# Low-rank attention: a row product in a key pair of banks ahead of the block of full products, and a fifth key tile that begins its chain afresh

## The chip, the cores and the metric

The program runs on one core of one Trainium2 chip. The metric is device microseconds of one execution. The engines are named PE (TensorE matmul), PEld (its weight loads), DVE (VectorE), ACT (ScalarE), POOL (GpSimd) and SP (SyncE, which here only issues DMAs).

## What is computed

The input x is (8, 1024, 128) in float32. Six residual layers follow one another, each after a layer norm:

```python
    x = x + 0.5 * _L0_ffn_ref(_layernorm(x, axis=-1), ...)
    x = x + _L0_attn_ref(_layernorm(x, axis=-1), ...)
    x = x + 0.5 * _L0_ffn_ref(_layernorm(x, axis=-1), ...)
    x = x + 0.5 * _L1_ffn_ref(_layernorm(x, axis=-1), ...)
    x = x + _L1_attn_ref(_layernorm(x, axis=-1), ...)
    x = x + 0.5 * _L1_ffn_ref(_layernorm(x, axis=-1), ...)
```

The change is in the fifth, the low-rank attention with 8 heads over 1024 positions in each of 8 batches. Its front, as the reference has it:

```python
        c_q = h_t @ W_DQ + b_DQ
        c_kv = h_t @ W_DKV + b_DKV
        q_c = (c_q @ W_UQ + b_UQ).reshape(b, s, N_HEADS, D_K).transpose(0, 2, 1, 3)
        k_c = (c_kv @ W_UK + b_UK).reshape(b, s, N_HEADS, D_K).transpose(0, 2, 1, 3)
```

After it come a softmax over all 1024 keys, the weighing of the values and the product with W_O. The kernel absorbs the key weights into the query, so that a score is a product over KR = 64 numbers (32 latent, 32 rotary), the same keys for all heads of a batch.

## The kernel before

The stages run in the order a, w, b, c, m, d, for the six layers; m is the low-rank attention. The work of stage m is written out as a plan by low_rank_plan: a list of steps g, eight for each of 64 units u (8 batches by 8 heads; "head" below). Every engine walks through the same plan (pe_low_rank, act_low_rank, dve_low_rank, pool_low_rank) and takes its part of each step; semaphores order the engines among themselves.

In step g = 8u + t the key tile t of head u is scored against all 1024 queries: pe_key_scores writes [128 keys x 1024 queries] into a key pair of banks, pair 0 for even and pair 1 for odd tiles (side 0 and side 1 are the two halves of the queries). act_exponentials takes the exponential of the pair, and a pair is free for tile g + 2 when that is done (key_exp). Products are split into high and low parts of f32r. Tiles 0 and 1 have four terms: key high by query high, key low by query high, key high by query low, and the shift, a row of ones by q_shift, which subtracts each query's maximum. Tiles 2 to 7 don't start the bank anew. They add to the scores of tile t - 2, still in the bank, the product with the difference of the two key tiles (step_high, and its low part in key_low), three terms, and the shift stays in.

The maxima come from row products: pe_row_scores multiplies 128 queries by 512 keys for each side into one of the pairs 2 and 3, and dve_row_max reduces the pair to two maxima per partition. Eight row products serve one head; row r is issued at step g = r - ROW_LEAD, thirteen steps ahead, one in each step. After the eighth, dve_row_top reduces them, pool_shift makes shift_cols of it on GpSimd, and SP moves that into q_shift by eight DMAs of 128 numbers (sync_move_shift). q_shift and shift_cols have one buffer each. SP's order is: set for head u, then the four transfers of o_norm of head u - 2 (sync_move_head), and a store of a batch once in eight heads. PE waits for the set at the fourth term of tile 0 (shift_ready).

At t = 3 (BURST) of each head the block of full products follows the key tile on PE: the query product of a head ahead, one or two items (projections, transposes, low-rank features, differences and so on), the totals of the head before (pe_totals) and its weighing (pe_weigh), and then the row product. Items, weighing and row products take the pairs 2 and 3 in turn; each waits until the use before the last of the list is done (pair_free). On DVE the order of that step is: q_low, first item, norm work, reciprocal of the totals, second item, o_norm, row maximum.

## Time and profile before

| what | value |
| --- | --- |
| median of 3 runs | 1689.36 us (1688.67 to 1693.62) |
| the profiled execution | 1689.08 us, its span 1687.2 us |
| PE busy | 1549.9 us (92%) |
| DVE busy | 1282.9 us (76%) |
| ACT busy | 1044.0 us (62%) |
| POOL busy | 1018.0 us (60%) |
| DMA queue of SP | 21.0% of the 16 engines |

The span is the profiled execution from first to last instruction; the run's own time has some 2 us around it. Stage m covers roughly 600 to 1650 us. In the timelines a row is a run of like instructions: start, duration, engine, line, operation, output and input tile, count, and in brackets how long the engine had been idle and what released it. A name's buffer number is left out, so "pair" stands for all four pairs of banks.

### The profile page before, as it was taken

The numbers are of one execution on the slowest core, as the hardware profiler recorded it, in microseconds if no ns is written. First come the engines' busy times: TensorE is split into PE (matmuls) and PEld (weight loads), VectorE is DVE, ScalarE is ACT, GpSimd is POOL, SyncE is SP. The second block draws the span as 40 slices with busy tenths as digits, with TensorE's granted clock in tenths as the row PEclk, the third lists the DMA queues.
The fourth block names the chain that finished last, engine by engine and source line by source line (L and its number), as shares of the span: only waits on it lengthen the run. The fifth ranks groups of instructions, "written<-read, shape, count | busy, mean of one in ns | idle before, by whom it ended". The sixth has DMA issues, their size and how long they took to land.

```text
span 1687.2 us, 42461 instructions
## 1 busy us (share of the span) xinstructions
PE 1549.9 (92%) x16971; PEld 1071.7 (64%) x16971; DVE 1282.9 (76%) x2345; ACT 1044.0 (62%) x1670; POOL 1018.0 (60%) x727
## 2 busy tenths in 40 slices
PE   4669999999987789999999999999999999999995
PEld 3557777777766546666666666666666666666664
DVE  5656777776669678788888888888887888887862
ACT  5447777778757436656665756656665666565562
POOL 5300111100026539778888888888888888887882
PEclk9879999999978779999999999999999999999998
DMA  4465566765200000000000010010010001001001
GB/s 132 119 165 143 144 163 154 177 149 151 60 30 1 1 1 11 10 9 11 8 12 10 9 23 9 11 20 12 8 24 9 10 10 22 11 8 23 8 12 44
DMA packets 198681, 81.63 MB, mean 48 GB/s; under 512 B 152552, under 2 KB 177492, under 8 KB 198356
## 3 DMA queue, kind: packets, MB, share of 16 engines
q1 hardware_dynamic: 198484, 78.93, 21.0%
q8 instruction: 133, 2.18, 0.6%
q14 instruction: 64, 0.52, 0.1%
HBM read 39.79 MB, written 29.88 MB: 41 GB/s over the span
## 4 chain that ended last, share of the span: by engine, by line
PE 58%; POOL 2%; DVE 2%; ACT 2%; issue 1%; SPq 0%; DMA 0%; ACTq 0%; DVEq 0%; POOLq 0%
PE pair L1930 23%; PE pair L1984 13%; PE pair L1859 7%; PE pair L1971 5%; PE pair L1676 2%; PE pair L1665 1%; ACT prob L1943 1%; DVE amax L1869 1%; PE pair L1690 1%; PE pair L1718 1%; PE pair L1705 1%; POOL w_mix L1956 1%; PE pair L1667 1%; PE pair L1700 1%; POOL Wm L1956 1%
## 5 line engine op out<-in xcount | busy, mean ns | idle before, releaser
L1943 ACT ACTIVATE prob<-pair 128x1024 f32<-128x1024 f32 x512 | 511.4, 1026 | 357.1 <-PE pair L1930 335.1
L1869 DVE TENSOR_REDUCE amax<-pair 128x2 f32<-128x1024 f32 x512 | 586.4, 1218 | 17.7 <-PE pair L1859 17.2
L1956 POOL TENSOR_TENSOR w_mix<-w_mix,prob 128x1024 f32<-128x1024 f32 x128 | 305.9, 2390 | 33.8 <-ACT prob L1943 26.0
L1956 POOL TENSOR_TENSOR Wm<-Wm,prob 128x1024 f32<-128x1024 f32 x124 | 296.4, 2390 | 24.5 <-ACT prob L1943 17.3
L523 POOL TENSOR_SCALAR veps<-mv 128x8 f32<-128x8 f32 x47 | 11.4, 243 | 425.8 <-DVE mv L496 424.2
L1189 DVE TENSOR_REDUCE mx_neg<-pair 128x4 f32<-128x512 f32 x256 | 164.9, 687 | 91.0 <-PE pair L1093 90.3
L1984 PE MATMUL pair<-prob,values 128*32 128x256 f32 x4096 | 233.7, 380 | 0.0
L1859 PE MATMUL pair<-key_high,q_hi 64*128 64x512 f32 x1024 | 223.2, 431 | 11.1 <-DVE amax L1869 5.0
L1930 PE MATMUL pair<-q_hi,key_low 64*128 64x512 f32 x1024 | 202.6, 390 | 0.0
L1984 PEld LDWEIGHTS pair<-prob,values 128*32 128x32 f32 x4096 | 129.6, 110 | 92.9 <-issue 10.7
L1139 ACT ACTIVATE yT<-pair 128x512 f32<-128x512 f32 x256 | 138.6, 593 | 69.8 <-PE pair L1045 67.6
L1930 PE MATMUL pair<-q_hi,step_high 64*128 64x512 f32 x768 | 172.3, 442 | 4.1 <-ACT prob L1943 1.7
L1859 PEld LDWEIGHTS pair<-key_high,q_hi 64*128 64x128 f32 x1024 | 97.8, 187 | 88.1 <-DVE amax L1869 36.8
L1930 PE MATMUL pair<-q_low,step_high 64*128 64x512 f32 x768 | 153.3, 392 | 0.0
L545 ACT ACTIVATE y<-x,mean_neg,rstd 128x128 f32<-128x128 f32 x336 | 134.8, 484 | 18.4 <-POOL mean_neg L531 18.4
L1994 DVE RECIPROCAL o_inv<-pair 128x256 f32<-128x256 f32 x64 | 111.5, 1743 | 33.4 <-PE pair L1971 33.0
L1930 PEld LDWEIGHTS pair<-q_hi,step_high 64*128 64x128 f32 x768 | 72.6, 184 | 78.2 <-ACT prob L1943 67.1
L1930 PEld LDWEIGHTS pair<-q_hi,key_low 64*128 64x128 f32 x1024 | 98.1, 186 | 7.6
L1093 PE MATMUL pair<-keys,queries 64*128 64x128 f32 x1024 | 99.8, 316 | 0.0
L1045 PE MATMUL pair<-queries,keys 64*128 64x128 f32 x1024 | 96.1, 307 | 0.0
L1953 POOL TENSOR_TENSOR w_mix<-prob 128x1024 f32<-128x1024 f32 x32 | 76.2, 2380 | 29.4 <-ACT prob L1943 29.4
L2001 DVE TENSOR_TENSOR o_norm<-pair,o_inv 128x256 f32<-128x256 f32 x64 | 27.1, 424 | 80.4 <-issue 40.6
(229 smaller groups left out, 2667.6 us busy)
## 6 DMA issues: line engine op xcount, KB each, us to landing
rows_mem<-once SPq DMA_DIRECT2D x128, 128.0 KB, 2.0
queries<-rows_mem SPq DMA_DIRECT2D x64, 256.0 KB, 4.6
keys<-rows_mem SPq DMA_DIRECT2D x16, 1024.0 KB, 7.1
rows_mem<-once SPq DMA_DIRECT2D x128, 64.0 KB, 1.9
q_shift<-shift_cols SPq DMA_DIRECT2D x512, 0.5 KB, 2.0
yT<-o_norm SPq DMA_DIRECT2D x256, 32.0 KB, 1.8
x<-x_dram SPq DMA_DIRECT2D x8, 512.0 KB, 7.2
out_dram<-x SPq DMA_DIRECT2D x7, 512.0 KB, 3.4
```

What stands on the lines that cost most here:

```text
L545: ins = e.activation(y_of(stage, b)[:, t, :], x[:, b * NT + t, :], ACT.Identity, bias=mean_neg[:, k, t:t + 1], scale=rstd[:, k, t:t + 1])
L1045: ins = e.matmul(key_shared_bank(n, r)[:, q * P:(q + 1) * P], keys[rows, b % 2, q, k0:k0 + 2 * W], queries[rows, hb % QUERY_BUFS, q, m].re ...
L1093: ins = e.matmul(bank(S_BANKS[r])[:, q * P:(q + 1) * P], queries[rows, hb % QUERY_BUFS, q, m].rearrange("p s w -> p (s w)"), keys[rows, b ...
L1139: e.activation(pT[:, u % P_TURNED].rearrange("p q k -> p (q k)"), key_shared_bank(*divmod(u, 2)), ACT.Exp).then_inc(*exps.up(u))
L1189: e.tensor_reduce(mx_neg[:, hb % 2, r, :, m], bank(S_BANKS[r]).rearrange("p (q k) -> p q k", q=QUADS), AX_X, ALU.max, negate=True).then_in ...
L1859: ins = e.matmul(bank(2 * places_m["row", r][0] + side), q_hi[rows, k, t * P:(t + 1) * P], key_high[rows, b % 2, half * HALF:(half + 1) * ...
L1869: e.tensor_reduce(amax1[:, u % 2].rearrange("p (s t) k -> p s t k", s=2)[:, :, t, half], pair[places_m["row", r][0]][:, :].rearrange("p (s ...
L1930: ins = e.matmul(banks[side], weights[rows, :], moving[rows, n, :], start=t < 2 and part == 0, stop=part == len(terms) - 1, skip_group_che ...
L1943: e.activation(prob1[:, g % P_BUFS, :], pair[g % 2][:, :], ACT.Exp, scale=SCALE1).then_inc(*key_exp.up(g))
L1956: e.tensor_tensor(into, into, p, ALU.add).then_inc(*summed_keys.up(g))
L1984: done = e.matmul(weighed[q * DC:(q + 1) * DC, 0:QUARTER], values[:, b % 2, t, :], part[:, q * QUARTER:(q + 1) * QUARTER], start=t == 0, s ...
L1994: e.reciprocal(o_inv[:, :], weigh_banks(u)[1][:, 0:QUARTER]).then_inc(*o_inverse.up(u))
```

## The change

The eighth row product of a head (and with it the maximum and the top reduction) is taken to step t = 3 as an early row, ahead of the block. On PE it comes right after key tile 3 and writes into the pair of tile 2 (pair 0), after its exponential. The step t = 7 has no row product any more (NO_ROW), and rows 4 to 7 of a head are issued a step later in the plan than before. Since pair 0 no longer holds the scores of tile 2, tile 4 is "fresh" like tiles 0 and 1: it waits for the early row's maximum, starts the bank anew, and has four terms, the shift among them. So SP, before it writes q_shift for head u, waits for tile 4 of head u - 1 instead of tile 1. The low part of tile 4's keys is made directly (an extra 128 columns in the "low" item's second half, on DVE and ACT), and the differences are made for tiles 2, 3, 5, 6, 7 only. The early row has place 0 with an empty list of earlier uses, so it waits for no use of pairs 2 and 3.

```diff
@@ -229,11 +229,23 @@
 ROW_PAIRS = 2, 3
 SUMMED = 6
 SHIFT_LAG = 0
-EARLY_ROWS = ()
+NO_ROW = 4
+FRESH = 0, 1, BURST + 1
+CHAINED = [t for t in range(NT) if t not in FRESH]
 
 
 NORM_WORK = (("m stats", None), ("m aggregate", None), ("m tiles", None), (None, "d stats"),
              (None, "d aggregate"), (None, "d tiles"), (None, "d scales"), (None, "d rounding"))
+
+
+def rows_at(g, count):
+
+    u, n = divmod(g + ROW_LEAD, NT)
+    if n == NO_ROW:
+        return None, None
+    before = NT * u + n - (n > NO_ROW)
+    early, row = (before - 1 if n == 0 else None), before
+    return tuple(r if r is not None and 0 <= r < count else None for r in (early, row))
 
 
 def low_rank_plan():
@@ -274,9 +286,14 @@
         copies, items, work, query, weigh = [], [], [], None, None
         if g % NT == BURST:
             copies, held = held, []
-        row = g + ROW_LEAD if 0 <= g + ROW_LEAD < NT * U else None
+        early, row = rows_at(g, NT * U)
         b, n = divmod(g, NT * NH)
         final = [FINAL[n]] if b == B and n in FINAL else []
+        if early is not None:
+            if g < 0:
+                use(("row", early), [("row", early, 0)])
+            else:
+                places["row", early] = 0, []
         if g % NT == BURST:
             items = items_at(b, g // NT % NH) if b >= 0 else []
             work = work_at(b, g // NT % NH) if 0 <= b < B else []
@@ -291,7 +308,7 @@
         if row is not None:
             use(("row", row), [("row", row, 0)])
         held = items if items else held
-        steps.append((g, features, copies, final, row, work, query, weigh, items))
+        steps.append((g, features, copies, final, early, row, work, query, weigh, items))
     return opening, opening_banks, steps, places
 
 
@@ -1701,9 +1718,10 @@
                          skip_group_check=True).then_inc(*low_done.up((a, i)))
             elif kind == "diff":
                 e.wait_ge(*y_stepped.at(a))
+                steps = chained_tiles(i)
                 for side in range(2):
-                    ins = e.matmul(bank(j)[side * KR:(side + 1) * KR, 0:3 * P], w_low[:, 0:KR],
-                                   y_step[:, i * 3 * P:(i + 1) * 3 * P], start=True, stop=True, skip_group_check=True)
+                    ins = e.matmul(bank(j)[side * KR:(side + 1) * KR, 0:steps.stop - steps.start], w_low[:, 0:KR],
+                                   y_step[:, steps.start - 2 * P:steps.stop - 2 * P], start=True, stop=True, skip_group_check=True)
                 ins.then_inc(*step_done.up((a, i)))
             elif kind == "const":
                 e.wait_ge(*set_low.at("ones"))
@@ -1747,7 +1765,9 @@
                 e.wait_ge(*step_done.at((a, i)))
                 if a >= 2:
                     e.wait_ge(*key_scored.at((64 * (a - 1) - 1, 1)))
-                e.activation(step_high[:, a % 2, i * 3 * P:(i + 1) * 3 * P], bank(j)[:, 0:3 * P], ACT.Copy).then_inc(
+                steps = chained_tiles(i)
+                e.activation(step_high[:, a % 2, steps.start - 2 * P:steps.stop - 2 * P],
+                             bank(j)[:, 0:steps.stop - steps.start], ACT.Copy).then_inc(
                     *step_high_done.up((a, i)))
             elif kind == "quant":
                 e.wait_ge(*xd_turned.at(("d", a, i)))
@@ -1755,15 +1775,24 @@
                     e.wait_ge(*products.at(("d", a - 1, 1)))
                 e.activation(d_turned[:, sl], bank(j), ACT.Copy).then_inc(*xd_copied.up(("d", a, i)))
 
+        def fresh_tiles(i):
+
+            tiles = [t for t in FRESH if t // (NT // 2) == i]
+            return slice(tiles[0] * P, (tiles[-1] + 1) * P)
+
+        def chained_tiles(i):
+
+            return slice(CHAINED[0] * P, FRESH[-1] * P) if i == 0 else slice((FRESH[-1] + 1) * P, T)
+
         def act_low_after(e, item):
 
             kind, a, i = item
             sl = slice(i * HALF, (i + 1) * HALF)
             if kind == "low":
                 e.wait_ge(*low_high_done.at((a, i)))
-                if i == 0:
-                    e.wait_ge(*keys_done.at((a, i)))
-                    e.activation(key_low[KR:P, a % 2, 0:2 * P], key_low[0:KR, a % 2, 0:2 * P].bitcast(F32), ACT.Copy)
+                e.wait_ge(*keys_done.at((a, i)))
+                e.activation(key_low[KR:P, a % 2, fresh_tiles(i)], key_low[0:KR, a % 2, fresh_tiles(i)].bitcast(F32),
+                             ACT.Copy)
                 e.activation(key_high[KR:P, a % 2, sl], key_high[0:KR, a % 2, sl].bitcast(F32), ACT.Copy).then_inc(
                     *key_copied.up((a, i)))
 
@@ -1794,16 +1823,17 @@
                 e.wait_ge(*low_high_done.at((a, i)))
                 ins = e.scalar_tensor_tensor(out=cq[KR:QR, k, sl], in0=bank(j)[KR:QR, :], scalar=b_dq[DC:KR],
                                              in1=cq[DC:KR, k, sl].bitcast(F32), op0=ALU.add, op1=ALU.subtract)
-                if i == 0:
-                    ins = e.scalar_tensor_tensor(out=key_low[0:KR, k, 0:2 * P], in0=bank(j)[0:KR, 0:2 * P],
-                                                 scalar=b_low[0:KR], in1=key_high[0:KR, k, 0:2 * P].bitcast(F32),
-                                                 op0=ALU.add, op1=ALU.subtract)
+                fresh = fresh_tiles(i)
+                ins = e.scalar_tensor_tensor(out=key_low[0:KR, k, fresh],
+                                             in0=bank(j)[0:KR, fresh.start - i * HALF:fresh.stop - i * HALF],
+                                             scalar=b_low[0:KR], in1=key_high[0:KR, k, fresh].bitcast(F32),
+                                             op0=ALU.add, op1=ALU.subtract)
                 ins.then_inc(*keys_done.up((a, i)))
             elif kind == "diff":
                 e.wait_ge(*step_high_done.at((a, i)))
-                cols = slice(i * 3 * P, (i + 1) * 3 * P)
-                e.tensor_tensor(key_low[:, k, 2 * P + i * 3 * P:2 * P + (i + 1) * 3 * P], bank(j)[:, 0:3 * P],
-                                step_high[:, k, cols], ALU.subtract).then_inc(*steps_ready.up((a, i)))
+                steps = chained_tiles(i)
+                e.tensor_tensor(key_low[:, k, steps], bank(j)[:, 0:steps.stop - steps.start],
+                                step_high[:, k, steps.start - 2 * P:steps.stop - 2 * P], ALU.subtract).then_inc(*steps_ready.up((a, i)))
             elif kind == "const":
                 e.wait_ge(*const_done.at(a))
                 if a >= 2:
@@ -1827,8 +1857,12 @@
                     e.wait_ge(*step_done.at((a - 1, 1)))
                 else:
                     e.wait_ge(*mla_product.at("bias"))
-                e.tensor_tensor(y_step, yT[:, a % 2, W + 2 * P:W + T], yT[:, a % 2, W:W + T - 2 * P],
-                                ALU.subtract).then_inc(*y_stepped.up(a))
+                for half in range(2):
+                    steps = chained_tiles(half)
+                    ins = e.tensor_tensor(y_step[:, steps.start - 2 * P:steps.stop - 2 * P],
+                                          yT[:, a % 2, W + steps.start:W + steps.stop],
+                                          yT[:, a % 2, W + steps.start - 2 * P:W + steps.stop - 2 * P], ALU.subtract)
+                ins.then_inc(*y_stepped.up(a))
 
         def pool_add_bias(e, a):
             xs = x[:, a * NT:(a + 1) * NT, :]
@@ -1838,7 +1872,8 @@
                 *bias_added.up(a))
 
         def pair_free(e, use):
-            for held in places_m[use][1] or [None]:
+            before = places_m[use][1]
+            for held in [None] if before is None else before:
                 low_bank_free(e, held)
 
         def row_tiles(r):
@@ -1894,7 +1929,7 @@
 
             e.wait_ge(*shift_steps.at((u, 2)))
             if u:
-                e.wait_ge(*key_scored.at((NT * (u - 1) + 1, 1)))
+                e.wait_ge(*key_scored.at((NT * (u - 1) + FRESH[-1], 1)))
             else:
                 e.wait_ge(*set_low.at("shift rows"))
             for t in range(NT):
@@ -1913,7 +1948,9 @@
                 e.wait_ge(*steps_ready.at((b, 1)))
             if g >= 2:
                 e.wait_ge(*key_exp.at(g - 2))
-            if t < 2:
+            if t == BURST + 1 and (u + 2) * NT <= total:
+                e.wait_ge(*row_maxed.at((u + 2) * NT - 1))
+            if t in FRESH:
                 terms = (key_high[:, b % 2, ks], q_hi), (key_low[:, b % 2, ks], q_hi), \
                     (key_high[:, b % 2, ks], q_low), (ones_shift[:, :], q_shift)
             else:
@@ -1927,7 +1964,7 @@
                 for side in range(2):
                     rows = slice(side * KR, (side + 1) * KR)
                     n = 0 if moving is q_shift else k
-                    ins = e.matmul(banks[side], weights[rows, :], moving[rows, n, :], start=t < 2 and part == 0,
+                    ins = e.matmul(banks[side], weights[rows, :], moving[rows, n, :], start=t in FRESH and part == 0,
                                    stop=part == len(terms) - 1, skip_group_check=True)
                     if part == len(terms) - 1:
                         ins.then_inc(*key_scored.up((g, side)))
...
@@ -2063,6 +2096,10 @@
                     e.wait_ge(*x_dve.at(("c", B - 1)))
                 if 0 <= g < total:
                     pe_key_scores(e, g)
+                if early is not None:
+                    if g >= 0:
+                        e.wait_ge(*key_exp.at(g - 1))
+                    pe_row_scores(e, early)
                 if query is not None or items:
                     pair_free(e, ("items", g))
                 if query is not None:
@@ -2075,15 +2112,13 @@
                     if query is not None:
                         low_bank_free(e, ("query", query, 0))
                     pe_low_part(e, item, item_bank(g, n))
-                if row is not None and early_row(g):
-                    pe_row_scores(e, row)
                 if weigh is not None:
                     pe_weigh(e, weigh)
-                if row is not None and not early_row(g):
+                if row is not None:
                     pe_row_scores(e, row)
 
         def act_low_rank(e):
-            for g, features, copies, final, row, work, query, weigh, items in plan_m:
+            for g, features, copies, final, early, row, work, query, weigh, items in plan_m:
                 if g == LAST_C["copy"]:
                     act_c_turned(e, B - 1)
                 elif g == STEPS_AT + 1:
...
@@ -2142,6 +2177,9 @@
                     dve_opening(e, "diff")
                 for part, half in final:
                     dve_final(e, part, half)
+                if early is not None:
+                    dve_row_max(e, early)
+                    dve_row_top(e, early // NT)
                 if query is not None:
                     dve_low_part(e, ("query", query, 0), item_bank(g, 1))
                 for n, item in enumerate(items[:1]):
@@ -2152,20 +2190,14 @@
                     dve_invert_totals(e, weigh)
                 for n, item in enumerate(items[1:], start=1):
                     dve_low_part(e, item, item_bank(g, n))
-                if row is not None and early_row(g):
-                    dve_row_max(e, row)
-                    if row % NT == NT - 1:
-                        dve_row_top(e, row // NT)
                 if weigh is not None:
                     dve_normalise(e, weigh)
-                if row is not None and not early_row(g):
+                if row is not None:
                     dve_row_max(e, row)
-                    if row % NT == NT - 1:
-                        dve_row_top(e, row // NT)
 
         def pool_low_rank(e):
             work_before = []
-            for g, features, copies, final, row, work, query, weigh, items in plan_m:
+            for g, features, copies, final, early, row, work, query, weigh, items in plan_m:
                 for item in features:
                     pool_low_after(e, item)
                 for part, half in final:
...
```

## Rows read from the trace of the kernel before

**Rows 1.** The page: span, busy share of PE, granted clock in 40 slices.

```profile
span 1687.2 us, 42461 instructions
...
PE 1549.9 (92%) x16971; PEld 1071.7 (64%) x16971; DVE 1282.9 (76%) x2345; ACT 1044.0 (62%) x1670; POOL 1018.0 (60%) x727
...
PEclk9879999999978779999999999999999999999998
```

**Rows 2.** Busy time by stretch: sixty heads; then PEclk, DMA share, GB/s.

```profile
647.20:1627.25 980.05, 973.22 (x10158) 618.44 (x10154) 813.66 (x1028) 607.55 (x743) 833.05 (x506) 1.00 0.09 13
```

**Rows 3.** Timeline of PE over one head.

```profile
1129.48 0.40 PE L1930 MATMUL pair<-q_shift,ones_shift 64*128 64x512 f32 x2
1129.72 0.39 PE L1859 MATMUL pair<-key_high,q_hi 64*128 64x512 f32 x2
...
1132.83 0.40 PE L1930 MATMUL pair<-q_low,step_high 64*128 64x512 f32 x2
1133.15 0.50 PE L1665 MATMUL pair<-cq,w_query 98*128 98x512 f32 x1
...
1140.67 0.40 PE L1930 MATMUL pair<-q_low,step_high 64*128 64x512 f32 x2
```

**Rows 4.** Timeline of ACT, exponentials of the same head.

```profile
1125.41 1.94 ACT L1943 ACTIVATE prob<-pair 128x1024 f32<-128x1024 f32 x2 [3.31 <-PE pair L1930]
...
1131.18 2.04 ACT L1943 ACTIVATE prob<-pair 128x1024 f32<-128x1024 f32 x2
...
1141.24 1.94 ACT L1943 ACTIVATE prob<-pair 128x1024 f32<-128x1024 f32 x2 [4.25 <-PE pair L1930]
```

**Rows 5.** Timelines of DVE and POOL in the same head.

```profile
1124.67 9.14 DVE L1869 TENSOR_REDUCE amax<-pair 128x2 f32<-128x1024 f32 x8
...
1134.92 0.21 POOL L1891 TENSOR_TENSOR shift_cols<-ccol,shift 128x8 fp32r<-128x8 f32 x1
```

**Rows 6.** Timeline of SP's queue: sets of eight shift transfers, opening and stage.

```profile
605.88 5.06 SPq L1902 DMA_DIRECT2D q_shift<-shift_cols  x8
...
647.20 5.71 SPq L1902 DMA_DIRECT2D q_shift<-shift_cols  x8
...
692.55 5.03 SPq L1902 DMA_DIRECT2D q_shift<-shift_cols  x8
...
1135.15 6.33 SPq L1902 DMA_DIRECT2D q_shift<-shift_cols  x8
1141.52 2.50 SPq L2012 DMA_DIRECT2D yT<-o_norm  x4
...
1627.25 5.72 SPq L1902 DMA_DIRECT2D q_shift<-shift_cols  x8
```

**Rows 7.** What SP's queue waited for: us in total, times, longest.

```profile
SPq L1902 <- POOL shift_cols L1891: 349.6, 64, 85.5
SPq L1897 <- PE pair L1930: 217.1, 63, 4.5
```

**Rows 8.** The chain of waits through the first set, opening.

```profile
610.33 2.00 DMA q_shift<-shift_cols
...
612.38 0.80 PE pair L1930 x2
```

**Rows 9.** Timeline of PE in the layers before the stage.

```profile
538.92 1.32 PE L1321 MATMUL pair<-cst,prob 128*128 128x128 f32 x8 [2.34 <-POOL prob L1261]
540.03 3.40 PE L630 MATMUL pair<-w_mix,yT 128*128 128x128 f32 x16
...
548.86 1.09 PE L1321 MATMUL pair<-cst,prob 128*128 128x128 f32 x8 [1.53 <-POOL prob L1261]
549.79 1.95 PE L630 MATMUL pair<-w_mix,yT 128*128 128x128 f32 x16
```

**Rows 10.** Busy time by stretch, as rows 2.

```profile
536.00:544.00 8.00, 5.66 (x33) 5.05 (x31) 7.84 (x16) 7.51 (x17) 6.65 (x8) 0.79 0.00 1
```

**Rows 11.** Who waited for whom, 640 to 1640 us.

```profile
PEld pair L1859 <- DVE amax L1869: 29.4, 121, 0.5
```

More of the change, by code:

```diff
@@ L2040, in pe_low_weights @@
                          skip_group_check=True).then_inc(*mla_product.up("bo"))
-        def early_row(g):
-            return g % NT == BURST and g // NT % NH in EARLY_ROWS
         def item_bank(g, n):
@@ L2135, in dve_low_rank @@
         def dve_low_rank(e):
-            for g, features, copies, final, row, work, query, weigh, items in plan_m:
+            for g, features, copies, final, early, row, work, query, weigh, items in plan_m:
                 if g == CONST_AT + 1:
@@ L2154, in dve_low_rank @@
                     dve_low_part(e, item, item_bank(g, n))
-                if row is not None and early_row(g):
-                    dve_row_max(e, row)
-                    if row % NT == NT - 1:
-                        dve_row_top(e, row // NT)
                 if weigh is not None:
                     dve_normalise(e, weigh)
-                if row is not None and not early_row(g):
+                if row is not None:
                     dve_row_max(e, row)
-                    if row % NT == NT - 1:
-                        dve_row_top(e, row // NT)
         def pool_low_rank(e):
             work_before = []
-            for g, features, copies, final, row, work, query, weigh, items in plan_m:
+            for g, features, copies, final, early, row, work, query, weigh, items in plan_m:
                 for item in features:
```

## The prediction

> **What bounds the kernel now.** I read the page first: one execution of 1687.2 us, TensorE busy in 92% of it, its clock at full speed nearly throughout [rows 1]. Then the table by stretches for the sixty heads from 647.20 to 1627.25 us: TensorE busy 973 of 980 us, VectorE 814, GpSimd 833, ScalarE 608, DMA at 9%, clock 1.00 [rows 2]. So in the low-rank stage TensorE is the bound, and nothing else is close to full. Then the timeline of TensorE over one head [rows 3], those of ScalarE, VectorE and GpSimd beside it [rows 4, 5], and the SP queue [rows 6, 7], because the change touches a wait there.
>
> The head as the reader should see it: tile 0 of a head reaches its shift term at 1129.48, tile 3's last product is issued at 1132.83, the block of full products (query, transposes, totals, weighing) runs from 1133.15 until the row product and tile 4 follow it, and tile 4's last product starts at 1140.67 [rows 3]. A head lasts (1627.25 - 647.20) / 60 = 16.33 us by the starts of the shift transfers [rows 6]. I cut it in two at the moments that the change ties together:
> - from tile 4 scored to the next tile 0's shift term. The exponential that starts at 1125.41 after a wait for TensorE is that of tile 4, so 1129.48 - 1125.41 = 4.07 us [rows 3, 4].
> - the rest, from the shift term to the next tile 4 scored: 16.33 - 4.07 = 12.26 us on average. In the head shown it is 1141.24 - 1129.48 = 11.76 us [rows 3, 4], with two transposes as its items.
>
> **The wait that the change moves.** q_shift has one buffer. Before, tiles 0 and 1 read it, and SP may overwrite it for head u once tile 1 of head u-1 is scored. The change makes tile 4 a reader too, and SP now waits for tile 4 of head u-1. How much room is there? Now the set is started by GpSimd's shift_cols, not by TensorE: shift_cols starts at 1134.92 and SP's first transfer at 1135.15 [rows 5, 6]; SP's waits for TensorE before that end earlier, and each is followed by one for shift_cols [rows 7]. The set is eight transfers issued one after the other, and they are long: 57 sets that the SP queue shows whole last 5.03 to 6.33 us, 5.51 on average, first and last of them 647.20 and 1627.25 [rows 6]. What comes after the issue is seen in the opening, the one place where TensorE waits for a set: first issue 605.88 [rows 6], eighth at 610.33, 2.00 us to its landing, q_shift's matmul at 612.38 [rows 8]. The issue group there lasted 5.06 us [rows 6], so 612.38 - 605.88 = 6.50 is the group plus 1.44. On average then 5.51 + 1.44 = 6.95 us from tile 4 scored to the shift term, where 4.07 are available today. Today the 6.95 start at 1135.15 and end by about 1142.1 to 1143.5, and tile 0 needs them at about 1145.8 (1129.48 + 16.33): that cover, the block of full products, is gone when the set starts behind it.
>
> Behind the waiting shift term in TensorE's queue stand the row product, tiles 1 to 3 and the block; ScalarE and GpSimd run dry behind them. Behind the waiting SP stand the four o_norm transfers of head u-2 (and, once in eight heads, one store). They last 2.50 us [rows 6] and are wanted by the output projection one head later; set and move end 5.51 + 2.50 + about 2 us landing = 10 us after tile 4, the next block begins 6.95 + 3.67 (1133.15 - 1129.48) = 10.6 us after it. This is costed at nothing, with 0.6 us of cover; if that cover fails, it is a wait of about 1 us in seven heads.
>
> By the Trainium skill, "DMA: Bandwidth & Descriptors", section "Anatomy of one DMA", a transfer has a fixed cost of about 2.0 us of which the sequencer's dispatch is some 50 ns (given for the path through GpSimd); by that a set would be an estimated 8 x 0.05 + 2.0 = 2.4 us and would still fit. The trace disagrees with it on the issue: the issue group of eight took 5.06 us in the opening, 0.63 each [rows 6].
>
> **The other edits.**
> - Tile 4 gets a fourth term. Two matmuls on the two row halves follow the pair before at 0.24 us (1129.48 to 1129.72 [rows 3]): +0.23 us per head, in the 12.26.
> - The early row goes into a key pair ahead of the block. The product itself (0.23) leaves the stretch behind tile 7 and comes before the block. It must wait for the exponential of tile 2, which is the second of the two that start at 1131.18 and end at 1133.22 [rows 4]; TensorE would be there at 1133.07. So 0.15 waited and 0.23 computed, +0.38 in the 12.26. What is left out behind tile 7 lies now in the stall and saves nothing; if there were no stall it would save up to 0.23.
> - VectorE has one row maximum less between blocks and one more at the block. Eight maxima run without a gap for 9.14 us [rows 5]; with a stall in each head VectorE is idle in part, so that relief buys nothing. The early maximum (1.22) and the top reduction delay q_low by at most 0.4 us, within the 0.38 already counted. Bound: nothing to 0.4 more.
> - Once per batch: the difference products lose a third of their first half, an extra 128-column subtraction and copy come in, and GpSimd's y_step is two instructions. A few hundred ns on engines with room, eight times: nothing. In the opening, rows 4 to 7 come a step later: 1 us at most.
>
> **The sum.** New head: 12.26 + 0.23 + 0.38 + 6.95 = 19.82 us, against 16.33: +3.49. It applies to heads 1 to 63: 63 x 3.49 = 220 us. TensorE then stands still for 6.95 less its work from tile 4 to the shift term (4.07 less at most 0.2 for the row that has gone, so 3.9): 3.0 us in every head.
>
> **What the idle stretch does to the clock.** Before the stage, TensorE waited 2.34 us for GpSimd and the clock then fell: 0.79 on average over 536 to 544 [rows 10], and the group of 16 products that begins at 540.03 took 3.40 us; after a wait of 1.53 us the same group took 1.95 [rows 9]. A fall from 2.4 to 1.2 GHz thus cost 3.40 - 1.95 = 1.45 us. A gap of 3.0 us is longer than the one that was followed by a fall, but not each gap need be; I take three heads in four: 63 x 0.75 x 1.45 = 68 us. Bounds: none (0) and twice the price in each head (63 x 2.9 = 183). The work around these gaps is not that of the heads, which is why the lower bound stays.
>
> The Trainium skill, "TensorE: Matmul & The Clock Gate", section "HAM oscillation — how this bites in real kernels", tells of a loop that waits for a DMA in every round and begins every round at the low clock, throttled time costing half of itself. It speaks against this change; rows 9 agree with it, for another cause of the wait.
>
> The profiled execution took 1689.08 us by its own time (span 1687.2), the median of the runs shown is 1689.36; so 1689 + 220 + 68 = 1977 us.
>
> **Rivals.**
> - Likeliest (0.58): stall with the clock falling in most heads, 1977; its own range 1925 to 2045.
> - The stall alone, the clock stays at 1.00 (0.27): 1689 + 220 = 1909. For it: in the heads TensorE is dense on either side of the gap. Against it: rows 9. With the shortest sets (5.03 each, 30 us less in all) 1879.
> - The clock stays low twice as long, or the sets are all of the longest kind (0.09): 1689 + 220 + 183 = 2092; sets of 6.33 alone would add 63 x 0.82 = 52.
> - The set ends in time and the new wait costs nothing (0.03): this decides itself where issue and landing together are under 3.9 us. Then the head costs 0.23 + 0.38 more and up to 0.23 less: 1689 + 63 x 0.38 = 1713. Rows 6 and 8 speak against it. It is where the skill's 50 ns would lead.
> - The other side, faster (0.02): the set ends in time and VectorE's relief counts. Its late maxima hold up TensorE's row weights by 29.4 us in the stage [rows 11]; without those and with the fourth term alone added (63 x 0.23 = 14.5) it would be 1689 - 29.4 + 14.5 = 1674. It, too, needs a set under 3.9 us. Within 0.3% of before (0.01) only where these two meet.
>
> **How the numbers follow.** The range runs from the stall without a fall and with some short sets, 1885, to most of the deeper fall, 2060; it leaves out some 0.05 + 0.05 at the ends and the 0.06 in which there is no stall. A change of 0.3% is about what a measurement of this kernel can tell from none. Faster 0.02, same 0.01, slower 0.97.
>
> **What would show it.** In the profile after: TensorE waiting for DMA q_shift in 63 heads, some 3 us each, about 190 us in all; SP's eight issues starting right after tile 4's products instead of after shift_cols; a head of about 20 to 21 us; TensorE's busy share down to some 80%; the granted clock below 1.00 in the stage; matmul groups of tiles 0 to 3 at 0.43 instead of 0.23 us a pair in many heads; no VectorE row maximum that TensorE waits for. The prediction is wrong if the set begins before tile 4 or takes under 4 us, if the wait for q_shift is short, or if the clock row reads 1.0 throughout (then 1909).

## The result and the profile after

The changed kernel takes 1970.47 us (median of 4 runs, 1966.82 to 1980.75), the kernel before 1691.49 us beside it: ratio 1.166, 95% interval 1.161 to 1.172. The forecast was 1977 us, range 1885 to 2060. The profiled execution has a span of 1965.0 us.

The page of the changed kernel, as [rows 1]; of the chain of waits only the two lines by engine and by line:

```profile
span 1965.0 us, 42748 instructions
...
PE 1655.0 (84%) x17099; PEld 1143.0 (58%) x17099; DVE 1296.6 (66%) x2353; ACT 1050.2 (53%) x1678; POOL 1016.8 (52%) x735
...
PEclk9799999999877989999889989989899999998998
...
PE 43%; SPq 14%; DMA 7%; ACT 4%; issue 2%; DVE 1%; POOL 0%; ACTq 0%; DVEq 0%; POOLq 0%
SPq L1937 14%; PE pair L1967 13%; PE pair L2021 12%; DMA q_shift<-shift_cols 7%; PE pair L1894 5%; PE pair L2008 5%; ACT prob L1980 4%; PE pair L1693 2%; PE pair L1682 1%; PE pair L1736 1%; PE pair L1707 1%; PE pair L1684 1%; PE pair L1717 1%; PE pair L1723 1%; PE pair L1700 0%
```

TensorE's share fell from 92% to 84%, and two entries in the chain that ended last belong to no computing engine: the issue of the shift transfers (L1937, 14%) and their landing (7%), a fifth of the span. The table by stretches over 61 heads, columns as [rows 2], shows the same loss spread over the whole stage, and the clock at 0.93 on average:

```profile
642.33:1907.36 1265.03, 1088.80 (x10436) 696.29 (x10434) 840.61 (x1048) 622.53 (x762) 845.39 (x521) 0.93 0.07 10
```

The timeline of SP's queue, as [rows 6]. A head is (1907.36 - 642.33) / 61 = 20.74 us:

```profile
642.33 5.47 SPq L1937 DMA_DIRECT2D q_shift<-shift_cols  x8
...
1203.10 5.03 SPq L1937 DMA_DIRECT2D q_shift<-shift_cols  x8
1208.17 2.50 SPq L2049 DMA_DIRECT2D yT<-o_norm  x4
...
1907.36 5.03 SPq L1937 DMA_DIRECT2D q_shift<-shift_cols  x8
```

And TensorE over one such head, as [rows 3], from tile 4's shift term (1202.59) to the early row and the query product:

```profile
1202.59 0.40 PE L1967 MATMUL pair<-q_shift,ones_shift 64*128 64x512 f32 x2
...
1206.99 0.40 PE L1967 MATMUL pair<-q_low,key_high 64*128 64x512 f32 x2
1209.59 0.79 PE L1967 MATMUL pair<-q_shift,ones_shift 64*128 64x512 f32 x2 [2.20 <-DMA q_shift<-shift_cols]
1210.18 0.63 PE L1894 MATMUL pair<-key_high,q_hi 64*128 64x512 f32 x2
1210.60 0.63 PE L1967 MATMUL pair<-q_hi,key_high 64*128 64x512 f32 x2
...
1214.94 0.50 PE L1894 MATMUL pair<-key_high,q_hi 64*128 64x512 f32 x2 [0.23 <-ACT prob L1980]
1215.37 0.50 PE L1682 MATMUL pair<-cq,w_query 98*128 98x512 f32 x1
```

The reader should see three things. Tile 4's shift term is issued at 1202.59 and SP begins its set at 1203.10, where before it began when shift_cols was ready [rows 5, 6]. TensorE has done three terms of tile 0 by 1207.4 and stands still until 1209.59, 6.49 us after the set's first issue. And after the gap the pairs follow at 0.42 us instead of the 0.23 of [rows 3]: 1210.18, 1210.60. That is the clock at 1.2 GHz: granted are 1.00 from 1205 to 1209.6 and 0.50 from 1209.6 to 1212.2. Such falls follow the gap in 35 of the 48 heads between 640 and 1640 us, and the clock is at its low level for some 150 of these 1000 us. The waits of 640 to 1900 us, as [rows 11]:

```profile
PEld pair L1967 <- DMA q_shift<-shift_cols: 174.3, 61, 4.1
PE pair L1967 <- DMA q_shift<-shift_cols: 147.8, 61, 3.7
```

Every one of the 61 heads waits, 2.9 us each by the weight loads, 2.4 by the matmuls.

### The profile page after: what moved, and what is told of

It reads as the page before. It is cut to its first block, busy times and chain, and to the rows that moved or that the text cites. A ratio compares the mean times of both kernels' runs of the same rounds, so it can differ in the third digit from the quotient of the medians.

```text
span 1965.0 us, 42748 instructions
## 1 busy us (share of the span) xinstructions
PE 1655.0 (84%) x17099; PEld 1143.0 (58%) x17099; DVE 1296.6 (66%) x2353; ACT 1050.2 (53%) x1678; POOL 1016.8 (52%) x735
## 4 chain that ended last, share of the span: by engine, by line
PE 43%; SPq 14%; DMA 7%; ACT 4%; issue 2%; DVE 1%; POOL 0%; ACTq 0%; DVEq 0%; POOLq 0%
SPq L1937 14%; PE pair L1967 13%; PE pair L2021 12%; DMA q_shift<-shift_cols 7%; PE pair L1894 5%; PE pair L2008 5%; ACT prob L1980 4%; PE pair L1693 2%; PE pair L1682 1%; PE pair L1736 1%; PE pair L1707 1%; PE pair L1684 1%; PE pair L1717 1%; PE pair L1723 1%; PE pair L1700 0%
## 5 line engine op out<-in xcount | busy, mean ns | idle before, releaser
L1904 DVE TENSOR_REDUCE amax<-pair 128x2 f32<-128x1024 f32 x512 | 608.4, 1223 | 319.5 <-PE pair L1894 315.8
L1894 PE MATMUL pair<-key_high,q_hi 64*128 64x512 f32 x1024 | 240.4, 466 | 11.2 <-DVE amax L1904 4.2
L540 POOL TENSOR_SCALAR veps<-mv 128x8 f32<-128x8 f32 x47 | 11.5, 245 | 427.7 <-DVE mv L513 426.3
L1967 PE MATMUL pair<-q_shift,ones_shift 64*128 64x512 f32 x384 | 100.4, 519 | 152.8 <-DMA q_shift<-shift_cols 152.8
L1967 PE MATMUL pair<-q_hi,key_low 64*128 64x512 f32 x1024 | 220.1, 426 | 0.0
L1894 PEld LDWEIGHTS pair<-key_high,q_hi 64*128 64x128 f32 x1024 | 111.6, 214 | 83.9 <-ACT prob L1980 29.8
L1967 PE MATMUL pair<-q_hi,step_high 64*128 64x512 f32 x640 | 151.4, 469 | 6.9 <-ACT prob L1980 1.7
L1967 PEld LDWEIGHTS pair<-q_shift,ones_shift 64*128 64x128 f32 x384 | 44.1, 226 | 188.2 <-DMA q_shift<-shift_cols 180.9
L1990 POOL TENSOR_TENSOR Wm<-prob 128x1024 f32<-128x1024 f32 x31 | 73.8, 2381 | 128.3 <-ACT prob L1980 128.3
L1967 PE MATMUL pair<-q_low,step_high 64*128 64x512 f32 x640 | 134.7, 416 | 0.0
L1967 PEld LDWEIGHTS pair<-q_hi,key_low 64*128 64x128 f32 x1024 | 110.0, 211 | 16.2
```

Source lines behind the costliest of these rows:

```text
L1894: ins = e.matmul(bank(2 * places_m["row", r][0] + side), q_hi[rows, k, t * P:(t + 1) * P], key_high[rows, b % 2, half * HALF:(half + 1) * ...
L1904: e.tensor_reduce(amax1[:, u % 2].rearrange("p (s t) k -> p s t k", s=2)[:, :, t, half], pair[places_m["row", r][0]][:, :].rearrange("p (s ...
L1967: ins = e.matmul(banks[side], weights[rows, :], moving[rows, n, :], start=t in FRESH and part == 0, stop=part == len(terms) - 1, skip_grou ...
L1990: e.tensor_tensor(into, prob1[:, (g - 1) % P_BUFS, :], p, ALU.add).then_inc(*summed_keys.up(g))
```

## The experiments

**The wait by itself.** The kernel before with one number changed:

```diff
-                e.wait_ge(*key_scored.at((NT * (u - 1) + 1, 1)))
+                e.wait_ge(*key_scored.at((NT * (u - 1) + BURST + 1, 1)))
```

> The kernel before, in which SP waits for tile 4 of head u-1 before it writes q_shift, instead of tile 1; tile 4 stays chained, no early row. Theory: this wait alone makes most of the loss. Head = 12.26 + 5.24 (mean set after the change) + 1.44 = 18.94 us, + 2.61 us x 63 = 164, and the clock falls add 60 to 75: 1915 to 1930 us. Rival, the transfers have room enough and the loss needs the new rows or the fourth term: 1690 to 1710 us.

Measured: 1910.6 us, ratio 1.132 (1.127 to 1.136). 61 heads wait for q_shift here too, 173.4 us by the weight loads. So 221 of the 280 us come from where SP waits, with none of the new products; the time is 4 us under the range of its theory. The clock is at 0.93 over 640 to 1640.

**The same edit one tile earlier.**

```diff
-                e.wait_ge(*key_scored.at((NT * (u - 1) + 1, 1)))
+                e.wait_ge(*key_scored.at((NT * (u - 1) + BURST, 1)))
```

> The kernel before, in which SP waits for tile 3 of head u-1, the last before the block, instead of tile 1. Theory: tile 3 is scored at 1133.3 in the head shown, before shift_cols is ready at 1135.13, so the wait costs nothing: 1689 us; it is the block of 6.7 us behind the wait, not the wait as such, that cost 222 us when the tile was tile 4. Rival: any later wait of SP delays the set: some 1700 to 1800 us.

Measured: 1690.97 us, ratio 1.001 (0.999 to 1.003). Tile 3 is free, tile 4 costs 221 us. In this run SP's queue shows whom it waits for:

```profile
SPq L1897 <- PE pair L1930: 357.0, 63, 6.7
SPq L1902 <- POOL shift_cols L1891: 211.2, 64, 85.2
```

The wait for TensorE has grown from 217.1 us [rows 7] to 357.0, and that for shift_cols has shrunk by as much, from 349.6 to 211.2. It still comes last. The later wait eats slack and no more.

**A second buffer for the shift.** The changed kernel, with room for the buffer made by moving o_norm:

```diff
-        q_shift = sb("q_shift", [P, 1, HALF], F32R, low)
+        q_shift = sb("q_shift", [P, 2, HALF], F32R, low)
...
-        o_norm = sb("o_norm", [P, 2, QUARTER], F32, low)
+        o_norm = Wm[:, 2 * T - 2 * P:2 * T + 2 * P].rearrange("p (k n) -> p k n", k=2)
...
-            if u:
-                e.wait_ge(*key_scored.at((NT * (u - 1) + FRESH[-1], 1)))
+            if u >= 2:
+                e.wait_ge(*key_scored.at((NT * (u - 2) + FRESH[-1], 1)))
...
-                    n = 0 if moving is q_shift else k
+                    n = u % 2 if moving is q_shift else k
```

> The changed kernel with a second full buffer of q_shift (o_norm moves into a part of the weight tile Wm that is no longer read), and SP waiting for tile 4 of head u-2. The shift term stays as it is in the changed kernel, 64 rows at stride one, so it lacks the surcharge that both earlier ways around the wait carried (0.2 us a pair over 32 rows, 0.22 us a pair at stride four, three pairs a head: 1791 - 57 = 1734 and 1763 - 42 = 1721). Theory: no wait for q_shift, clock 1.00, 1720 to 1735 us, what the early row and the fourth term cost by themselves. The forecast's value for this is 1713. Rival, relief of VectorE: 1690 or less.

Measured: 1734.9 us, ratio 1.028 (1.026 to 1.029). No wait for q_shift is left, and the clock is back at 1.00:

```profile
640.00:1640.00 1000.00, 973.96 (x10018) 614.46 (x10018) 805.12 (x1009) 604.44 (x737) 814.34 (x499) 1.00 0.08 12
```

236 us of the loss are the buffer's. The other 46 are the new products', more than the 24 (1713 - 1689) of the forecast.

**The second buffer under the kernel before** (the same edit there, after tile 1 of head u-2).

> The kernel before with the second buffer of q_shift and o_norm in Wm, the set still after tile 1 but of head u-2. Both theories: nothing, 1689 us within 0.3%, since before the set waits for shift_cols and not for the buffer. It tells whether the second buffer by itself gains or costs.

Measured: 1688.6 us, ratio 1.000 (0.999 to 1.001). The buffer and the place of o_norm are neutral.

**The fourth term without the early row.** As the run with the second buffer, and:

```diff
 def rows_at(g, count):
-    u, n = divmod(g + ROW_LEAD, NT)
-    if n == NO_ROW:
...
+    return None, g + ROW_LEAD if 0 <= g + ROW_LEAD < count else None
...
-            if t == BURST + 1 and (u + 2) * NT <= total:
-                e.wait_ge(*row_maxed.at((u + 2) * NT - 1))
...
                     dve_row_max(e, row)
+                    if row % NT == NT - 1:
+                        dve_row_top(e, row // NT)
```

> As the run with the second buffer, but all row products at their old places: no early row, tile 4 still afresh with four terms. Theory: 63 x 0.23 = 14.5 us over before, 1704 us; the difference to the run with the early row, 17 to 30 us, is the price of the early row. Rival: the term is hidden behind ScalarE's pace, 1690, and the early row is all of the rest.

Measured: 1697.7 us, ratio 1.005 (1.004 to 1.007), some 6 us under the 1704 expected. The term costs 9.3 us (6 to 11.5 by the interval), 0.15 a head, and the early row 1734.9 - 1697.7 = 37.2 us, 0.6 a head over the 63 that have one, more than the 17 to 30 us expected. TensorE's row weights waited 29.4 us for row maxima before [rows 11]; here, 640 to 1640 us again, it is 2.2. But the waits for ScalarE's exponentials are 107.9 instead of the 82.6 of before, nearly as much more:

```profile
PEld pair L1960 <- ACT prob L1973: 107.9, 299, 0.8
...
PEld pair L1889 <- DVE amax L1899: 2.2, 9, 0.4
```

So the wait has changed its cause and hardly its length. Added up over 58 heads, the time from the start of a row product to the start of the key tile after it is 149 us before and 149 us here, and the fourth term's own step is 13.4 us, its full 0.23 a head. Some 3 us come back, most of them inside the block; why is not shown.

Where the early row's 0.6 lie, the timelines of TensorE show. First without, then with the early row:

```profile
1205.17 0.40 PE L1960 MATMUL pair<-q_low,step_high 64*128 64x512 f32 x2
1205.50 0.50 PE L1677 MATMUL pair<-cq,w_query 98*128 98x512 f32 x1
```

```profile
1203.52 0.40 PE L1967 MATMUL pair<-q_low,step_high 64*128 64x512 f32 x2
1204.21 0.50 PE L1967 MATMUL pair<-q_hi,key_high 64*128 64x512 f32 x2 [0.29 <-ACT prob L1980]
...
1208.35 0.40 PE L1967 MATMUL pair<-q_low,step_high 64*128 64x512 f32 x2
1208.79 0.49 PE L1894 MATMUL pair<-key_high,q_hi 64*128 64x512 f32 x2
1209.22 0.50 PE L1682 MATMUL pair<-cq,w_query 98*128 98x512 f32 x1
1209.56 0.39 PE L1684 MATMUL pair<-cq,w_query 98*128 98x512 f32 x1
1209.79 0.60 PE L1713 MATMUL pair<-cst,y 128*128 128x128 f32 x4
```

From tile 3's last product to the query product it is 0.33 us without the early row and 0.87 with it, 0.54 more: 0.23 for the row itself, 0.21 of waiting (0.44 instead of 0.23 to the early row), and 0.10 because the query product follows the early row at 0.43 and tile 3 at 0.33. The place that the row has left, behind tile 7, gives nothing back: from tile 7's last product (1203.52) to tile 0 it takes 0.69 us, of which 0.29 are shown as a wait for the exponential. Over 58 heads the two runs have 39.7 us there with the row gone and 39.8 with the row in between, and 31.6 us more between tile 3 and the query product, 0.54 a head.

**Query product first.** As the run with the second buffer:

```diff
-                if early is not None:
-                    if g >= 0:
-                        e.wait_ge(*key_exp.at(g - 1))
+                if early is not None and g < 0:
                     pe_row_scores(e, early)
                 if query is not None or items:
                     pair_free(e, ("items", g))
                 if query is not None:
                     pe_low_part(e, ("query", query, 0), item_bank(g, 1))
+                if early is not None and g >= 0:
+                    e.wait_ge(*key_exp.at(g - 1))
+                    pe_row_scores(e, early)
```

> As the run with the second buffer, but TensorE computes the query product before the early row instead of after it; VectorE's order is kept. Theory: the wait for tile 2's exponential (0.1 to 0.3 us a head) is covered by the query product, 6 to 19 us less than the run with the second buffer. Rival: the early row's cost is its place between products of other shapes, not the wait: no difference, or more, since VectorE takes the early maximum before q_low and q_low now comes later.

Measured: 1749.3 us, ratio 1.034 (1.032 to 1.037), 14 us more than the second buffer alone. The theory was wrong. The row now stands between two products over all rows of the array:

```profile
1216.87 0.40 PE L1967 MATMUL pair<-q_low,step_high 64*128 64x512 f32 x2
1217.19 0.50 PE L1682 MATMUL pair<-cq,w_query 98*128 98x512 f32 x1
1217.53 0.40 PE L1684 MATMUL pair<-cq,w_query 98*128 98x512 f32 x1
1217.86 0.51 PE L1894 MATMUL pair<-key_high,q_hi 64*128 64x512 f32 x2
1218.29 0.66 PE L1713 MATMUL pair<-cst,y 128*128 128x128 f32 x4
```

It takes 0.33 us to reach it and 0.43 to leave it, where among its like the step is 0.23. The row's waits for the exponential are indeed gone (weight loads, 0.4 us instead of 28.6 in 640 to 1640), but the two passages eat the gain: from tile 3's last product to the first item it is 1.42 us here (1216.87 to 1218.29) and 1.44 with the row first (1208.35 to 1209.79). So up to the first item nothing is won and nothing is lost, and the 14 us lie behind it, in the block. There the second part of the rival shows, q_low coming later. First a wait of the run with the second buffer, then the same one here:

```profile
PEld pair L1713 <- DVE q_low L1813: 2.9, 7, 0.4
```

```profile
PEld pair L1713 <- DVE q_low L1813: 4.7, 7, 0.7
```

All such waits of weight loads for q_low between 640 and 1640 us come to 15.7 us, against 5.4. The rest is spread over the block and the row behind it in parts of 1 to 2 us and is not traced to a cause.

**Shorter set.** The changed kernel with two transfers:

```diff
-            for t in range(NT):
-                side, n = divmod(t, NT // 2)
-                e.dma_start(q_shift[side * KR:side * KR + 1, 0, n * P:(n + 1) * P].bitcast(F32).rearrange(
-                    "o (p t) -> o p t", t=1), shift_cols[:, t:t + 1].bitcast(F32)).then_inc(
-                    shift_moved, 16)
+            for side in range(2):
+                e.dma_start(q_shift[side * KR:side * KR + 1, 0, :].bitcast(F32).rearrange(
+                    "o (p t) -> o p t", p=P), shift_cols[:, side * NT // 2:(side + 1) * NT // 2].bitcast(
+                    F32)).then_inc(shift_moved, 16)
...
+                    across = moving[rows, n, :]
+                    if moving is q_shift:
+                        across = across.rearrange("r (p t) -> r t p", p=P)
```

> The changed kernel, with the shift set moved by two transfers of 128 x 4 numbers instead of eight of 128 x 1; q_shift is kept in order (p, t), and the shift term reads it with a stride of four numbers. The wait for tile 4 stays. Theory, the eight issues of 0.63 us are what is long: set = 2 x 0.63 + 1.44 = 2.7 us, under the 3.9 available, so no wait and about 1713 us, clock 1.00. Rival, what is long is the landing of 1024 single numbers: the set stays at 5 us or more and the time above 1850 us. If the strided read is slower, the shift term's matmuls (0.39 us at the high clock) show it, 3 pairs a head.

Measured: 1763.6 us, ratio 1.044 (1.040 to 1.048), with the wait for tile 4 still in place: far from the rival's 1850, and 51 us over the 1713 of its theory. The set is two issues, and TensorE no longer waits for it:

```profile
1215.39 1.17 SPq L1936 DMA_DIRECT2D q_shift<-shift_cols  x2
```

```profile
1214.66 0.62 PE L1969 MATMUL pair<-q_shift,ones_shift 64*128 64x512 f32 x2
1215.10 0.42 PE L1894 MATMUL pair<-key_high,q_hi 64*128 64x512 f32 x2
```

So the eight issues were the length of the set. The second fence is the price of this way out: read at a stride of four numbers, the shift term takes 0.44 us a pair (1214.66 to 1215.10) instead of 0.23, three times a head. 63 x 3 x 0.21 = 40 us, and 1763.6 - 40 = 1724 is near the 1734.9 of the second buffer; the 11 us between them are not explained.

**Two rows in one buffer.** The changed kernel, odd heads' shift at rows 32 and 96:

```diff
-            if u:
-                e.wait_ge(*key_scored.at((NT * (u - 1) + FRESH[-1], 1)))
+            if u >= 2:
+                e.wait_ge(*key_scored.at((NT * (u - 2) + FRESH[-1], 1)))
...
+                row = side * KR + u % 2 * DC
...
+                    if moving is q_shift:
+                        rows = slice(side * KR + u % 2 * DC, side * KR + (u % 2 + 1) * DC)
```

> The changed kernel, with the shift kept in two places: even heads at rows 0 and 64 of q_shift, odd heads at rows 32 and 96, the shift term over 32 rows instead of 64, and SP waiting for tile 4 of head u-2 instead of u-1. Everything else of the change stays. Theory of the moved wait: TensorE no longer waits for q_shift, the clock stays at 1.00 in the stage, and a head costs 16.33 + 0.23 + 0.38 less up to 0.23 = 16.7 us: about 1713 us. Rival, the early row and the fourth term themselves hold up the head (bank of tile 2, maximum before tile 4): well over 1800 us, with TensorE waiting for ScalarE or VectorE at the block. Second rival, VectorE's relief counts: 1674 us.

Measured: 1791.0 us, ratio 1.060 (1.056 to 1.064), between its two theories. The wait is gone, but the 1713 us were missed by 78, and most of that is the price of this way out. A term over 32 rows among terms over 64 costs more:

```profile
1200.96 0.40 PE L1970 MATMUL pair<-q_low,key_high 64*128 64x512 f32 x2
1201.28 0.50 PE L1970 MATMUL pair<-q_shift,ones_shift 32*128 32x512 f32 x2
1201.72 0.50 PE L1894 MATMUL pair<-key_high,q_hi 64*128 64x512 f32 x2
```

1200.96 to 1201.72 is 0.76 us for two pairs that take 0.46, 0.3 more, and that three times a head is 57 us: 1791 - 57 = 1734, as with the second buffer.

**The wait filled.** The changed kernel, with work for TensorE in the gap:

```diff
                 if t == 0 and part == 3:
+                    for _ in range(10 if u else 0):
+                        for side in range(2):
+                            zeros = slice(side * KR + DC, (side + 1) * KR)
+                            e.matmul(banks[side], ones_shift[zeros, :], q_shift[zeros, 0, :], start=False,
+                                     stop=False, skip_group_check=True)
                     e.wait_ge(*shift_ready(u))
```

> The changed kernel, with ten pairs of matmuls (32 rows x 512 columns, rows of q_shift that hold zeros, added to tile 0's banks) ahead of the wait for the shift term, some 2.2 us of TensorE work in the stretch in which it stood idle. The set is as late as before. Theory, the clock falls because of the idle stretch: with it filled the clock stays at 1.00 and the 187 us spent at 1.2 GHz in the stage cost nothing; by the periods that is 20.74 - 12.87 - 6.68 = 1.19 us a head, 75 us, so 1895 us. Rival, the falls have another cause or half of the loss is no matter of the clock: 1970 us. Where the wait is shorter than the filling, up to 0.3 us a head is lost again.

Measured: 1916.4 us, ratio 1.134 (1.130 to 1.138), 54 us less than the changed kernel although TensorE has more to do. The granted clock over 640 to 1640 is 0.99, where the changed kernel has 0.92; first the filled kernel, then the changed one:

```profile
640.00:1640.00 1000.00, 965.68 (x9516) 610.02 (x9516) 681.74 (x867) 512.23 (x631) 693.17 (x428) 0.99 0.07 10
```

```profile
640.00:1640.00 1000.00, 861.15 (x8234) 549.91 (x8228) 663.61 (x839) 494.09 (x607) 669.69 (x415) 0.92 0.07 10
```

The ten pairs last 2.56 us instead of the 2.2 counted. In one head the shift term behind them starts at 1223.62, where the set that began at 1216.91 was due at 1216.91 + 6.49 = 1223.40. If every head is like it, an overrun of 0.2 us a head is some 13 of the 21 us by which 1895 was missed; the five falls of the clock that are left between 640 and 1640 us are another part.

**The row in the block, in its own banks.** The kernel before with its switch on:

```diff
-EARLY_ROWS = ()
+EARLY_ROWS = tuple(range(8))
```

> The kernel before with its own switch for early rows on in all heads: at the block step the row product (and its maximum) comes after the items and totals and ahead of the weighing, in the pairs 2 and 3, instead of after the weighing. No fresh tile, no key pair, no moved wait. Theory from the runs so far, a row product costs TensorE its 0.23 us and about 0.2 us for each change between half-row and full-row products: before it stands beside tile 4 and makes no change of its own, here it makes two, 63 x 0.2 to 0.4 = 13 to 25 us slower than before. Rival: VectorE, given a maximum during the weighing, comes sooner through the next tiles and this pays for it: no change or faster.

Measured: 1826.0 us, ratio 1.080 (1.077 to 1.083). Slower, as the theory had it, but by 136 us and not by 13 to 25; its mechanism is too small. The waits tell what was left out, the banks:

```profile
PEld pair L1859 <- issue: 98.2, 51, 3.8
...
PE pair L1859 <- DVE x L1778: 32.8, 10, 3.4
PE pair L1859 <- DVE key_low L1805: 29.9, 13, 3.1
```

Inside the block the pairs 2 and 3 are held by the items, and the row waits until VectorE has finished with one. Over 58 heads the way from the last item or total to the weighing grows by 116 us, 2.0 a head. Such a wait lowers the clock too: it is at its low level for some 85 of the 1000 us between 640 and 1640 (0.96 granted, 1.00 before). By the changed kernel's rate, 65 us lost for some 187 at the low level, that would be an estimated 30 us of the 136; no run separates it. Against that the key pair of the change is the better place for an early row. But no run with an early row was faster than the kernel before.

## Why the prediction was right, step by step

| step | forecast | measured |
| --- | --- | --- |
| mean set, issue | 5.51 us | 5.24 us (57 sets shown whole) |
| first issue to shift term, beyond the set | 1.44 | 1.46 (6.49 - 5.03, one head) |
| shift term to tile 4 scored, clock 1.00 | 12.87 | 13.0 (second buffer) |
| the same, with the clock falls | 13.95 | 14.04 |
| head | 19.82 + 1.08 = 20.90 | 20.74 |
| stall per head | 3.0 | 2.4 (matmuls) to 2.9 (weight loads) |
| heads with a fall of the clock | three in four | 35 of 48 |
| clock falls, 63 heads | 68 us | 65 |

The 14.04 are the head less the set's way, 20.74 - 5.24 - 1.46. For the second buffer the head is 16.33 + (1734.9 - 1688.3) / 63 = 17.07, and less the 4.06 us from tile 4 scored to the shift term, which its timelines show unchanged, 13.0. The clock's share is 63 x (14.04 - 13.01) = 65 us; the filled wait gave 54 back with an overrun in it. The timelines of the two kernels, added up over 58 heads from product to product, say the same: the changed kernel is 216 us longer than the one with the second buffer, 157 of them at the wait for q_shift, and the other 60 (1.03 a head) are products that follow one another more slowly.

- The moved wait as the cause: shown from both sides. Alone in the kernel before it costs 221 us, taken out of the changed kernel it gives 236 back. The point that the prediction chose, that the set must not start behind the block of full products, is shown by tile 3 against tile 4: 1 us against 221.
- The set's length as eight issues: shown by the two transfers. The 50 ns of dispatch that the Trainium skill ("DMA: Bandwidth & Descriptors", section "Anatomy of one DMA") gives for the path through GpSimd would have left no wait. Here each issue on SP's queue took 0.63 us (5.03 / 8).
- The clock: shown by filling the gap. The rival without a clock fall (1909) was wrong, and the changed kernel without its falls would have lain at it: 1970 - 65 = 1905.
- The cover of the o_norm transfers (0.6 us): among the waits of 640 to 1900 us is none of TensorE for them; the cost of nothing holds.
- Of the signs, the wait for q_shift was put too high: about 190 us, where 61 heads show 148 (matmuls) to 174 (weight loads). TensorE's busy share is 84% and not some 80%.
- The new products: 24 us forecast at most (1713), 46 measured. The early row was mis-sized, +0.38 less up to 0.23 against 0.6. The 0.15 of waiting was 0.21. What was missing is the dearer passage from the row, a product over half the rows, to the query product over all of them, 0.43 us where tile 3 has 0.33. And the row taken from behind tile 7 gives nothing back, since ScalarE's exponentials set the pace there. The fourth term, 0.23 forecast, is 0.15 by the times; its step in the timeline is the full 0.23, and where the rest comes back is not shown.
- These misses pull against one another: sets 0.27 us shorter (17 us in all) and new products dearer by 0.14 in the stretch that counts (9 us). The forecast of 1977 was 6.5 us high. Part of its nearness is such luck.
- The rival of VectorE's relief (1674) was wrong in its mechanism and not only out of reach. The 29.4 us of waits for row maxima go away with the fourth term alone, and the kernel is 9.3 us slower and not 15 faster: waits for ScalarE, 25 us more, end just as late.

One thing stays open: why the long sets became fewer, 14 of 57 over 5.3 us after the change against 33 of 57 before. It goes with the place of the set and not with the new products. Of all 63 sets from the second on, 16 to 21 are that long in the three runs with the set behind tile 4 of the head before (the changed kernel, the wait by itself, the wait filled), and 34 to 37 in the kernel before, with the wait for tile 3, with two rows and with two buffers. What makes a single issue long no run shows.

## What to carry to other kernels

A reader added to a single-buffered tile moves the moment from which its next filling may start. Before the edit, find where that filling starts now and what ends last before it, and measure the whole way from the last reader to the next use. If a long block lies between the old last reader and the new one, it has been the cover for that transfer. A short product is priced by its neighbours' shapes and by the pace of whoever it waits for, and a place where the engine waits anyway returns nothing when the product leaves it. Nor is a wait worth its length if another one ends just as late.

## What the runs showed of the hardware

- A pair of shift terms reading 512 columns at a stride of four numbers takes 0.44 us, at stride one 0.23.
- A pair over 32 rows between pairs over 64 rows adds 0.3 us to the stream, though it has the same columns.
- A pair over half the rows that stands between products over all rows takes 0.33 us before it and 0.43 after it, 0.76 from product to product (the run with the query product first).
- One issue of 128 numbers on SP's queue takes 0.6 us, so eight in a row take some 5.0 us at least; two issues of 512 numbers take 1.17 us.
- With an idle gap of 1.9 to 3.7 us of TensorE in each head, the clock was at its low level for about 15% of 640 to 1640 us; with 2.56 us of products over 32 rows in the gap, 2%.
